# Six row buffers instead of four for the first layer's expert blocks, two of them in memory of the mask and of a bias

## What is computed

```python
logits = xn @ gate_w + gate_b
tw, ti = jax.lax.top_k(logits, K)                      # K = 2 of E = 6
tw = jax.nn.softmax(tw, axis=-1)
h = jax.nn.gelu(jnp.einsum('bsd,edh->besh', xn, ew1) + eb1[None, :, None, :], approximate=False)
eo = jnp.einsum('besh,ehd->besd', h, ew2) + eb2[None, :, None, :]
return jnp.einsum('bse,besd->bsd', w_full, eo)
```

## Time and profile before

| | |
|---|---|
| median of 3 runs | 706.04 us (705.33 to 708.42) |
| the profiled execution | 703.88 us, of which its span is 702.2 us |
| busiest engine over the span | TensorE, 623.0 us |
| stage of the 74 blocks, first transposition to last store's issue | 139.1 us to 250.2 us |
| of it, issue of load 9 to issue of load 73 | 149.64 us to 243.63 us |

### The profile page before, as it was taken

One profiled execution on the slowest core, in us unless ns is written; L12 is line 12 of the kernel. 1 busy time (PEld: TensorE's weight loads), 2 busy tenths in 40 slices (PEclk: granted clock), 3 DMA queues, 4 the chain that ended last, 5 costly groups with the idle time before them and its releaser, 6 DMA issues.

```text
span 702.2 us, 19558 instructions
## 1 busy us (share of the span) xinstructions
PE 623.0 (89%) x6221; PEld 442.9 (63%) x6222; DVE 494.8 (70%) x1302; ACT 414.2 (59%) x1144; POOL 445.5 (63%) x652
## 2 busy tenths in 40 slices
PE   4789989886988898995799999998999999999993
PEld 3667767675878775674354455556999855555442
DVE  5678785567667726999488888884444488887884
ACT  2565433443444454776766777875444377878793
POOL 6775888889038889993122487843333258878782
PEclk9999999999899999998999999999999999999997
DMA  8995111144467731110000011100222101111110
GB/s 250 281 298 157 41 43 59 44 111 102 91 108 140 139 69 34 34 33 5 1 32 1 13 32 32 35 25 20 69 69 71 54 25 43 33 32 32 32 47 16
DMA packets 69466, 48.34 MB, mean 69 GB/s; under 512 B 8011, under 2 KB 63750, under 8 KB 69382
## 3 DMA queue, kind: packets, MB, share of 16 engines
q1 hardware_dynamic: 62332, 34.09, 18.8%
q0 software_dynamic: 6144, 12.63, 7.4%
q10 hardware_dynamic: 906, 0.55, 0.3%
HBM read 24.00 MB, written 23.24 MB: 67 GB/s over the span
## 4 chain that ended last, share of the span: by engine, by line
PE 49%; DVE 15%; POOL 13%; issue 9%; ACT 7%; DMA 5%; DVEq 0%; SPq 0%; POOLq 0%; ACTq 0%
PE bank L1750 12%; PE bank L1012 7%; PE bank L1730 5%; PE bank L1821 5%; PE bank L1830 5%; POOL yg_first L1056 4%; ACT pb L1895 4%; DMA xg<-x_half 3%; DVE nmx L2062 3%; POOL spacer L1051 3%; PE bank L579 2%; PE bank L1116 1%; POOL pool_xy L365 1%; PE bank L1126 1%; PE bank L1712 1%
## 5 line engine op out<-in xcount | busy, mean ns | idle before, releaser
L1895 ACT ACTIVATE pb<-bank,nmx 128x512 f32<-128x512 f32 x256 | 173.6, 691 | 63.8 <-DVE nmx L2062 63.6
L2062 DVE TENSOR_REDUCE nmx<-bank 128x2 f32<-128x1024 f32 x128 | 155.2, 1216 | 14.6 <-PE bank L1750 13.9
L1230 ACT ACTIVATE turns<-bank,cols 128x128 f32<-128x128 f32 x148 | 46.4, 364 | 59.5 <-PE bank L1116 59.0
L1662 POOL TENSOR_TENSOR vs<-vt_first,rz 128x256 f32<-128x256 f32 x64 | 39.5, 617 | 61.4 <-DVE rz L2038 60.7
L1730 PEld LDWEIGHTS bank<-pb,vs 128*32 128x32 f32 x2048 | 54.1, 110 | 37.4 <-issue 22.2
L1730 PE MATMUL bank<-pb,vs 128*32 128x128 f32 x2048 | 68.9, 275 | 2.0 <-POOL vs L1662 2.0
L382 POOL DMA_INDIRECT x_half<-pool_xy,slot x64 | 62.5, 976 | 10.6 <-issue 10.6
L1750 PE MATMUL bank<-qk 64*128 64x512 f32 x256 | 65.6, 622 | 1.6 <-ACT pb L1895 1.5
L1750 PE MATMUL bank<-qk_first 64*128 64x512 f32 x256 | 64.3, 618 | 1.2 <-ACT qk_first L1282 0.7
L1662 POOL TENSOR_TENSOR vs<-vt,rz 128x256 f32<-128x256 f32 x64 | 39.3, 617 | 39.0 <-DVE rz L2038 34.7
L1695 POOL COPY xn_all<-w 128x512 f32 x39 | 24.0, 616 | 47.8 <-PE bank L1821 47.8
(11 more groups left out here) (275 smaller groups left out, 1442.2 us busy)
## 6 DMA issues: line engine op xcount, KB each, us to landing
y_half<-ys SPq DMA_DIRECT2D x74, 64.5 KB
x_half<-zero SPq DMA_DIRECT2D x2, 2368.0 KB, 17.6
xg<-x_half SPq DMA_DIRECT2D x74, 64.0 KB
x_sorted<-zero SPq DMA_DIRECT2D x1, 2496.0 KB, 18.6
xn_all<-x_sorted SPq DMA_DIRECT2D x39, 64.0 KB, 1.8
y_sorted<-xn_all SPq DMA_DIRECT2D x39, 64.0 KB, 1.6
x_all<-in_L_attn_x_dram SPq DMA_DIRECT2D x8, 256.0 KB, 6.1
w<-in_L_ffn_W_dram SPq DMA_DIRECT2D x1, 2048.0 KB, 12.4
```

What stands on the lines that cost most here:

```text
L1662: pool.tensor_tensor(vs[s][:, :, :], vt[bt % 2][:, n // 2 % TT, :, :].rearrange("p j d -> p (j d)") .unsqueeze(1).broadcast_to([P, 2, D]), ...
L1895: act.activation(pb[s + ab][:, :], psum[score_banks(k) + ab], ACT.Exp, bias=nmx[:, s + ab:s + ab + 1], scale=1.0, accum_out=zz[:, s + ab:s ...
L2062: dve.tensor_reduce(nmx[:, s:s + 2], banks[:, score_banks(k):score_banks(k) + 2, :], AX.X, ALU.max, negate=True).then_inc(n_mx, 1)
```

## The change

There are six row buffers instead of four. The two new ones are the tiles `cmask` and `bv_bc` of the attention. The loop of SyncE is the same text, but `NXG - 1` is now 5: five loads stand ahead of it, and turn `i` issues `load(i + 5)` and then `store(i - 3)`. Load 4, the first into one of the two tiles, waits for the end of the attention. `NY`, `LEAD` and the wait for store k - 9 stay as they are. The `o_ld` semaphores become six; to make room for them, `f_w`, which nothing used, goes, and `f_og` and `f_gg` are merged into one semaphore that counts both gate operations of a batch.

```diff
-        NXG = 4
-        xg0 = [sbe(f"xg0{i}", [P, D]) for i in range(NXG)]
+        NXG = 6
+        xg0 = [sbe(f"xg0{i}", [P, D]) for i in range(NXG - 2)] + [cmask, bv_bc]
...
-        f_w = sem("f_w")
...
-        f_og = sem("f_og")
...
-                act.activation(og[:, :], gt[:, :], ACT.Copy, bias=0.5, scale=-0.5).then_inc(f_og, 1)
+                act.activation(og[:, :], gt[:, :], ACT.Copy, bias=0.5, scale=-0.5).then_inc(f_gg, 1)
                 act.activation(gg[:, :], gt[:, :], ACT.Copy, bias=0.5, scale=0.5).then_inc(f_gg, 1)
...
             def first_part(bt):
-                act.wait_ge(f_og, bt + 1)
+                act.wait_ge(f_gg, 2 * bt + 1)
...
-                dve.wait_ge(f_gg, bt + 1)
+                dve.wait_ge(f_gg, 2 * bt + 2)
...
             def load(k):
                 if k in (0, NBH):
                     sp.wait_ge(t_sc0[k // NBH], 16 * 2 * NTH)
+                if k == NXG - 2:
+                    sp.wait_ge(a_os, B * TT + 2)
                 if k >= NXG:
                     sp.wait_ge(o_T, k - NXG + 1)
```

## The result

The changed kernel takes 774.79 us (median of 4 runs, 772.14 to 777.66) against 705.68 us of the kernel before in the same runs: a ratio of 1.0974, 95% interval 1.0916 to 1.1033, so 69 us slower. The forecast was 787 us, slower, in a range of 760 to 820 us. The profiled execution took 772.14 us, its span 770.5 us.

The account below looks back on a forecast made before the run. SyncE's queue was to become the bound, each load standing behind a store's landing: 84.7 us over 64 periods of 2.81 us, less 0.7 and 2.4, gives +81.6 us, so 787 us, range 760 to 820 us.

Parts of the forecast that it names:

- The wait moves right behind its store: SyncE's queue: load k still waits for store k - 9, now issued right ahead of it, so nothing overlaps the landing.
- The period as a sum of three: SyncE's queue: store to landing 2.35 us, landing to load 0.06, load to next store 0.40; 2.81 us, against 1.47 before.
- The landing: Time from a y_half store's issue until it has landed: taken as 2.35 us; mean between 1.95 and 2.85 us, chance 0.80.
- the last store's hand-over to GpSimd: After store 73: 2.35 us landing plus 0.27 us until GpSimd starts the second half's gathers; -2.4 us against before.
- Behind load 73: End of the blocks: block 73 comes alone, 5.8 us from load 73 to store 73 instead of 6.5 us; -0.7 us.
- The gathers: GpSimd: first half's 32 gathers, 51 us, done long before the last store; they would take gains made behind store 36.
- What was costed at nothing: Early loads, load 4's wait for the attention's end, load 37, merged semaphore, TensorE's lower clock, VectorE's stall: no cost, bar about 1 us.
- VectorE's stall: A VectorE stall like the one of 4.3 us vanishes, since finished blocks run several periods ahead of SyncE.
- No change: Rival: the landing stays hidden, needing it over in 1.0 us; 706 us, chance 0.03.
- faster: Rival: TensorE stops waiting for rows and the queue keeps pace; up to 6.9 us back, 699 us, chance 0.03.
- two other landings: Rivals on y_half stores: landing 1.6 us, towards 738 us, chance 0.07; landing 3.07 us, towards 834 us, chance 0.07.
- The signs: Profile after: 65 SyncE waits for stores, about 130 us instead of 4.0; TensorE waiting for rows in almost every block.

## Why the prediction was right, and by how much its size was off

**The wait moves right behind its store.** Right, and shown from both sides: the wait made short in the kernel before costs 73 us in the medians, and in the changed kernel the wait moved to VectorE, or put further from its store, gives all or nearly all of the loss back.

**The period as a sum of three.** Right in form. Landing to load is 0.06 us (0.02 + 0.02 + 0.03 us), as forecast; load to store is 0.36 to 0.37 us, not 0.40 us. The landing is the term that was mis-sized: 2.57 - 0.36 - 0.06 = 2.15 us in the mean of the stage, not 2.35 us. 65 x 0.20 = 13 us and 64 x 0.04 = 2.6 us are what the forecast had too much. Two other terms go against it: store 0 was issued 2.3 us later in this execution than in that of before, after an attention that the change doesn't touch (in the eight experiments it was issued between 145.7 and 151.7 us, with no relation to the edits: at 148.4 us with four plain buffers and the wait on VectorE, at 145.9 us with six buffers and the store first), and the last store's hand-over to GpSimd took 323.98 - 320.53 = 3.45 us, not 2.62 us. 81.6 - 13.0 - 2.6 + 2.3 + 0.8 = 69.1 us, against 68.9 us measured at GpSimd's gather.

Why 2.35 was too much is not fully known. It was read from two rows of a fuller queue, and with five buffers, where stores overlap loads and each other, the chain's stores took 2.89 us in the mean; that fits. But company is not all: with six buffers and the wait on VectorE, a store with loads issued 0.7 us ahead of it and 0.4 us behind it landed in 1.50 us:

```profile
197.97 1.50 DMA y_half<-ys
```

The landing also differs along the stage, as SyncE's waits of the changed kernel show in four stretches (150 to 171.5 us beside the scatter, 171.5 to 238 with GpSimd all but silent, 238 to 290 beside the gathers, 290 to 315 with it silent again):

```profile
SPq L1450 <- DMA y_half<-ys: 14.2, 8, 2.7
SPq L1450 <- DMA y_half<-ys: 42.2, 27, 3.2
SPq L1450 <- DMA y_half<-ys: 34.2, 18, 2.6
SPq L1450 <- DMA y_half<-ys: 18.3, 11, 2.4
```

That is 1.78, 1.56, 1.90 and 1.66 us a wait. A wait begins when the store's own issue is over, so it is about 0.45 us shorter than the landing. Beside the gathers it is some 0.3 us longer, which makes the landing there 2.35 us, as forecast; but the stretches with GpSimd silent hold 38 of the 64 waits and lie lower. The estimate from the Trainium skill's page "DMA: Bandwidth & Descriptors", section "Anatomy of one DMA", 2.15 us, came out on the measured mean, though its fit is for another path of issue.

**Behind load 73.** Forecast 5.8 us to store 73; measured 320.53 - 314.73 = 5.80 us. That the sum is exact is luck: the load landed in 1.73 us instead of 2.35 us, and the block took 4.07 us behind it instead of 3.44 us. The block did not come alone: TensorE still had products of the blocks ahead of it to do (L1114 and L1124), and waited once for VectorE (L1347).

**The gathers.** Right twice: in the changed kernel the first half's are long done, and with six buffers and the wait on VectorE they keep most of a stage that is 10 us shorter from arriving at the end.

**What was costed at nothing.** Right for the tiles and the semaphore (ratio 1.0016), and for VectorE's stall: SyncE waited 1.7 us for finished blocks from 150 to 315 us. TensorE's granted clock fell as expected and stayed all but hidden (below).

**The rivals.** No change and faster would have needed a landing below 1.0 us; the shortest of these stores took 1.7 us. Of the two other landings, 1.6 us and 3.07 us, neither is the mean; the measured one, 2.15 us, lies between them. The ceiling named for the faster case, 6.9 us, holds for the variants that keep rows five or four blocks ahead and take the wait out of their way: they gain 2 to 4 us.

**The signs.** All 65 waits were there, with 110.2 us instead of the 130 us named. TensorE waited for rows in 48 of 74 blocks, not in almost every one.

## What to carry to other kernels

When a queue runs further ahead, look at every wait that travels with what is moved: what counts is how much of the queue stands between an issue and the wait for it, and here it went from two loads and two stores to nothing while the wait's text did not change. One load and one store between them left a loss of 1.2 to 1.6%, two of each left none. The landing, about 2 us here, can be covered by more store buffers, by the order of the two lines, or by putting the wait on the engine that overwrites the buffer, which comes to it late. And before rows are fetched earlier, ask what takes over: of the 10 us by which the stage ended earlier, less than half was left at the second half's gathers.

## What the runs showed of the hardware

- The landing of a store of 128 rows of 516 bytes is no fixed number. In the changed kernel, with one store and one load at a time, the tile's row (`ys`) gives least, median and most:

```profile
DMA to landing us min/median/max: 1.7/2.0/3.7
```

  In the kernel before single ones took 2.30 and 3.07 us, and with five buffers 2.07 to 3.60 us. Beside GpSimd's gathers the changed kernel's chain has these, against 1.87 and 1.92 us in its calm stretch above:

```profile
242.13 2.52 DMA y_half<-ys
...
245.08 2.67 DMA y_half<-ys
```

- TensorE's granted clock fell with its idle time. In the calm stretch of the changed kernel (columns as in rows 8) it was 0.79 with 43.18 us busy of 66.5 us, where it was 1.00 in the busy stretch before; it cost next to nothing, since the queue's period, 2.57 us in the mean, was longer than a block's products at either level: 1.17 us at the full one (32.83 us for 28 blocks), and 1.93 us a block from 178.6 to 182.4 us, where TensorE caught up without a break at a granted clock of 0.51 (177 to 182.7 us). The stretch behind load 73, where TensorE was busy 8.62 of 9.20 us, was at 0.95.

```profile
171.50:238.00 66.50, 43.18 (x250) 37.82 (x248) 28.87 (x84) 17.54 (x56) 5.81 (x5) 0.79 0.20 55
...
314.70:323.90 9.20, 8.62 (x50) 6.57 (x49) 3.12 (x14) 3.94 (x9) 0.00 (x0) 0.95 0.25 72
```
